# FFN steps: the next step's maxima and indices in the middle of a step, and the gathering of indices on GpSimd

## The reference

```python
sim = jnp.einsum('pbnhd,hkpd->pbnhk', q, keys)          # 2 halves x 8 heads x 32 keys
sx, ix = jax.lax.top_k(sim[0], TOPK)                    # TOPK = 8
sy, iy = jax.lax.top_k(sim[1], TOPK)
all_scores = (sx[..., :, None] + sy[..., None, :]).reshape(b, n, H, TOPK * TOPK)
all_indices = (ix[..., :, None] * NUM_KEYS + iy[..., None, :]).reshape(b, n, H, TOPK * TOPK)
scores, pk = jax.lax.top_k(all_scores, TOPK)
indices = jnp.take_along_axis(all_indices, pk, axis=-1)
wd = down_embed[indices]
wu = up_embed[indices]
h = gelu_new(jnp.einsum('bnd,bnhkd->bnhk', x, wd))
h = jax.nn.softmax(scores, axis=-1) * h
out = jnp.einsum('bnhk,bnhkd->bnd', h, wu)
```

## Time and profile before

| | kernel before |
|---|---|
| median of 3 executions | 1291.11 us |
| the profiled execution | 1291.46 us |
| its span, first to last instruction | 1289.7 us |
| PE busy | 1153.1 us (89%) |
| DVE busy | 1133.3 us (88%) |
| ACT busy | 876.8 us (68%) |
| POOL busy | 641.1 us (50%) |
| mean granted TensorE clock | 0.906 |

### The profile page before, as it was taken

How to read it: one execution, slowest core, us unless ns; L and a number is a source line. 1 busy time by engine, 2 the same in 40 slices (tenths; PEclk the granted TensorE clock), 3 DMA queues, 4 the chain that set the end, 5 groups by cost and what they waited for, 6 DMA issues and landing times. The chain is left out here.

```text
span 1289.7 us, 32620 instructions
## 1 busy us (share of the span) xinstructions
PE 1153.1 (89%) x12726; PEld 899.9 (70%) x12726; DVE 1133.3 (88%) x2851; ACT 876.8 (68%) x1227; POOL 641.1 (50%) x545
## 2 busy tenths in 40 slices
PE   6669899999999999999999999999997739888878
PEld 4537677777767777776777777677776628778778
DVE  7776799998999999899999989998986689999984
ACT  4858798888889888888988888898874332222211
POOL 5435667757576775757677575767241300000000
PEclk9789999999999999999999999999999676666666
DMA  4149799999999999999999999998996300000000
GB/s 161 25 103 200 165 197 191 194 186 201 199 199 200 197 193 195 195 198 205 194 195 194 194 195 199 175 201 169 196 189 133 86 0 2 5 6 6 5 5 6
DMA packets 665506, 185.73 MB, mean 144 GB/s; under 512 B 653923, under 2 KB 662279, under 8 KB 665223
## 3 DMA queue, kind: packets, MB, share of 16 engines
q1 hardware_dynamic: 665350, 183.64, 74.0%
HBM read 19.44 MB, written 0.82 MB: 16 GB/s over the span
## 5 line engine op out<-in xcount | busy, mean ns | idle before, releaser
L1021 ACT ACTIVATE e<-ps,bias 128x1444 f32<-128x1444 f32 (+1 forms) x208 | 305.7, 1470 | 136.0 <-DVE bias L1098 135.1
L1220 PE MATMUL ps<-pT,xa_hi 128*128 128x128 f16 x2288 | 382.0, 217 | 16.3 <-ACT uT L1044 16.2
L1224 PE MATMUL ps<-pT,xa_hi 128*128 128x128 f16 x2288 | 381.8, 217 | 3.4 <-DMA pT<-p 3.4
L1221 PE MATMUL ps<-pT,xa_lo 128*128 128x128 f16 x2288 | 382.1, 217 | 0.0
L1096 DVE TENSOR_REDUCE nmax<-ps 128x1 f32<-128x1444 f32 (+1 forms) x208 | 343.8, 1653 | 23.9 <-PE ps L1204 22.8
L1108 DVE TENSOR_TENSOR p<-e,p 128x1408 f16<-128x1408 f32 (+3 forms) x288 | 302.5, 1091 | 37.5 <-ACT p L1029 36.8
L1029 ACT ACTIVATE p<-e 128x1408 f16<-128x1408 f32 (+1 forms) x208 | 287.9, 1384 | 17.3 <-DMA pT<-p 3.7
L971 POOL TENSOR_TENSOR p<-e,p 128x1408 f16<-128x1408 f32 (+1 forms) x128 | 196.7, 1558 | 187.3 <-ACT p L1029 187.3
L1220 PEld LDWEIGHTS ps<-pT,xa_hi 128*128 128x128 f16 x2288 | 222.5, 98 | 43.4 <-issue 30.1
L1202 PE MATMUL ps<-xT_hi,q_hi 128*128 128x512 f16 (+1 forms) x624 | 230.8, 370 | 7.4 <-PEq L40 3.8
L1221 PEld LDWEIGHTS ps<-pT,xa_lo 128*128 128x128 f16 x2288 | 222.5, 98 | 13.1 <-issue 0.2
(11 more groups left out here) (248 smaller groups left out, 1920.1 us busy)
## 6 DMA issues: line engine op xcount, KB each, us to landing
raw<-in_ctx SPq DMA_DIRECT2D x16, 704.0 KB
pT<-p SPq DMA_TRANSPOSE x416, 3.7
f_wq<-in_L_ffn_w_q SPq DMA_DIRECT2D x1, 1024.0 KB, 5.3
f_wqt<-in_ffn_wq_t SPq DMA_DIRECT2D x2, 512.0 KB, 7.7
raw<-in_ctx SPq DMA_DIRECT2D x48, 18.0 KB
x_tok<-in_x SPq DMA_DIRECT2D x4, 200.0 KB
out_x<-ost SPq DMA_DIRECT2D x6, 128.0 KB, 1.8
wk_d<-in_wk_d SPq DMA_DIRECT2D x1, 512.0 KB, 5.8
```

The lines of the kernel that those rows point to most:

```text
L1021: act.activation(e32[t % E_BUF][rows, :], score_banks(t)[rows, 0:T], ACT.Exp, bias=bias[rows, t % N_BUF:t % N_BUF + 1]).then_inc(e_done, 1)
L1220: pe.matmul(out, hi, ph, start=n == 0, stop=False)
L1221: pe.matmul(out, lo, ph, start=False, stop=False)
L1224: pe.matmul(out, hi, pl, start=False, stop=False)
```

## The change

In `ffn`:

- The multiply of the mask by `idxw` and the three sums go from DVE to POOL (`gathered`), with the semaphore `gather` between them. POOL's order becomes `gathered(i)`, `norm_rstd(i-2)`, `combine(i+1)`; before it was `combine(i)`, `norm_rstd(i-2)`.
- All maxima, all indices and the cast to `idxf` of step i+1 now stand inside step i on DVE, between `weigh(i-1, 1)` and the wait for POOL's sums, and behind it: 32 maxima, 20 indices (`AHEAD`), and behind `sel` the other 12 and the cast. Those of step 0 stand ahead of the loop, in an order by halves of the tokens instead of halves of the scores.
- The four `weigh` and the parts of the last norm are spread anew over the step.
- ACT runs `picks(i)` first in a step, and `hidden(i, 1)` and `last_norm(i-2)` behind `esc`, ahead of `rT`.

In `front`, the load of `side` counts on `ld_k` with `wk_d` and `wq_t`, for which everything that waits for one of the three now waits, and `kb_done` is merged into `const_chain`.

The diff, cut to its core:

```diff
-        LD_W, LD_LATE, LD_K = 16 * 2, 16 * 2, 16 * 2
+        LD_W, LD_LATE, LD_K = 16 * 2, 16 * 2, 16 * 3
...
-            pool.wait_ge(ld_side, 16)
-            pool.tensor_scalar(sc1[:, :, :], side[:, :, :], 1.0, 1.0 / QA_SCALE, ALU.add, ALU.mult).then_inc(kb_done, 1)
+            pool.wait_ge(ld_k, LD_K)
+            pool.tensor_scalar(sc1[:, :, :], side[:, :, :], 1.0, 1.0 / QA_SCALE, ALU.add, ALU.mult).then_inc(const_chain, 1)
...
+            def gathered(i):
+                nh, w = step_shape(i)
+                na = nh * NB
+                pool.wait_ge(pick, 3 * i + 3)
+                pool.wait_ge(wide_idx, i + 1)
+                pool.tensor_tensor(out=eq[0:w, 0:na, :, :], in0=eq[0:w, 0:na, :, :], in1=idxw[0:w, 0:na, :, :], op=ALU.mult).then_inc(gather, 1)
+                pool.wait_ge(gather, 3 * i + 1)
+                pool.tensor_tensor(out=half4[0:w, 0:na, :, :], in0=eq[0:w, 0:na, 0:4, :], in1=eq[0:w, 0:na, 4:8, :], op=ALU.add).then_inc(gather, 1)
...
+            combine(0)
+            wide_rows(1)
             for i in range(NSTEP):
-                combine(i)
-                if i == 0:
-                    wide_rows(1)
+                gathered(i)
                 if i >= 2:
                     norm_rstd(i - 2)
+                if i + 1 < NSTEP:
+                    combine(i + 1)
...
             def picks(i):
-                act.wait_ge(pick, 7 * i + 1)
+                act.wait_ge(idxf_done, i + 1)
+                if i:
+                    act.wait_ge(gather, 3 * i - 2)
...
+                picks(i)
                 hidden(i, 0)
-                if i >= 2:
-                    last_norm(i - 2)
-                hidden(i, 1)
-                picks(i)
                 if i + 1 < NSTEP:
                     sims_out(i + 1)
                 act.wait_ge(dsc_done, i + 1)
                 act.activation(esc[0:w, 0:nh, :, :], dsc[0:w, 0:nh, :, :], ACT.Exp).then_inc(esc_done, 1)
+                hidden(i, 1)
+                if i >= 2:
+                    last_norm(i - 2)
                 act.wait_ge(selT_ps, i + 1)
...
-                dve.wait_ge(wide_idx, i + 1)
-                dve.wait_ge(pick, 7 * i + 4)
-                dve.tensor_tensor(out=eq[0:w, 0:na, :, :], in0=eq[0:w, 0:na, :, :], in1=idxw[0:w, 0:na, :, :], op=ALU.mult).then_inc(pick, 1)
                 dve.wait_ge(soft_done, 3 * i + 2)
...
+                if i:
+                    weigh(i - 1, 1)
+                if i >= 2:
+                    norm_stats(i - 2, 0)
+                if i + 1 < NSTEP:
+                    next_maxima(i + 1)
+                if i >= 2:
+                    norm_stats(i - 2, 1)
+                if i + 1 < NSTEP:
+                    next_indices(i + 1, 0)
+                if i >= 2:
+                    norm_stats(i - 2, 2)
+                if i:
+                    weigh(i - 1, 2)
                 dve.wait_ge(sel_done, 4 * i + 1)
...
                 dve.tensor_copy(sel[0:w, 0:2, 0:nh, :], erc[0:w, :, 0:nh, :]).then_inc(sel_done, 1)
+                if i + 1 < NSTEP:
+                    next_indices(i + 1, 1)
+                    next_cast(i + 1)
+                if i >= 2:
+                    norm_shift(i - 2)
                 if i:
                     weigh(i - 1, 3)
-
-                if i + 1 < NSTEP:
-                    dve.wait_ge(sim_done, i + 1)
-                    for n in range(EARLY):
-                        dve.max(top[0:step_shape(i + 1)[1], 0, n, :], simb[0:step_shape(i + 1)[1], 0, n, :])
-
                 dve.wait_ge(selT_done, 3 * i + 1)
...
+            next_maxima(0)
+            for part in range(2):
+                next_indices(0, part)
+            for k in range(1, NG):
+                centred(k)
+            dve.wait_ge(narrow_done, 1)
+            next_cast(0)
```

More of the change, by code:

```diff
@@ L82, in front @@
         ld_x = [sem(f"ld_x{c}") for c in range(NG)]
-        ld_w, ld_late, ld_k, ld_side = (sem(n) for n in ("ld_w", "ld_late", "ld_k", "ld_side"))
+        ld_w, ld_late, ld_k = (sem(n) for n in ("ld_w", "ld_late", "ld_k"))
         const_chain = sem("const_chain")
@@ L94, in front @@
         kf_ps, kf_done, qa_ps, qa_hi_done, qa_lo_done = (sem(n) for n in ("kf_ps", "kf_done", "qa_ps", "qa_hi_done", "qa_lo_done"))
[L95 removed]
+        kb_ps, kbar_done = sem("kb_ps"), sem("kbar_done")
         q0_ps, q0_taken, q0_hi = sem("q0_ps"), sem("q0_taken"), sem("q0_hi")
@@ L278, in q0_out @@
                 if g == 0:
-                    act.wait_ge(kb_done, 2)
+                    act.wait_ge(const_chain, 13)
                 for j in range(4):
@@ L1256 @@
 NSTEP = -(-NT // STEP_TOK)
-EARLY = 6
+AHEAD = 20
 PAD = P + 4
@@ L1340, in ffn @@
         sim_ps, sim_done, top_done, comb_done, best_done = (sem(n) for n in ("sim_ps", "sim_done", "top_done", "comb_done", "best_done"))
+        idxf_done, gather = sem("idxf_done"), sem("gather")
         dsc_done, esc_done, pick, sel_done, selT_ps, selT_done = (sem(n) for n in ("dsc_done", "esc_done", "pick", "sel_done", "selT_ps", "selT_done"))
@@ L1430, in norm_rstd @@
                 pool.tensor_tensor(out=frs[0:w, 0:nh], in0=fve[0:w, 0:nh], in1=nhalf[0:w, 0:nh], op=ALU.pow).then_inc(z_rstd, 1)
+            def gathered(i):
[6 more added lines that the diff above has]
+                pool.tensor_tensor(out=half4[0:w, 0:na, :, :], in0=eq[0:w, 0:na, 0:4, :], in1=eq[0:w, 0:na, 4:8, :], op=ALU.add).then_inc(gather, 1)
+                pool.wait_ge(gather, 3 * i + 2)
+                pool.tensor_tensor(out=half2[0:w, 0:na, :, :], in0=half4[0:w, 0:na, 0:2, :], in1=half4[0:w, 0:na, 2:4, :], op=ALU.add).then_inc(gather, 1)
+                pool.wait_ge(gather, 3 * i + 3)
+                pool.tensor_tensor(out=ij[0:w, 0:nh, :, :].rearrange("s a n k -> s (a n) k"), in0=half2[0:w, 0:na, 0, :], in1=half2[0:w, 0:na, 1, :],
+                                   op=ALU.add).then_inc(sel_done, 1)
+            combine(0)
+            wide_rows(1)
             for i in range(NSTEP):
-                combine(i)
-                if i == 0:
-                    wide_rows(1)
+                gathered(i)
                 if i >= 2:
                     norm_rstd(i - 2)
+                if i + 1 < NSTEP:
+                    combine(i + 1)
             norm_rstd(NSTEP - 2)
@@ L1631, in norm_shift, with next_maxima, next_indices, next_cast @@
                                          op0=ALU.mult, op1=ALU.mult).then_inc(fnm_done, 1)
+            def next_maxima(i):
+                nh, w = step_shape(i)
+                if i:
+                    dve.wait_ge(sim_done, i)
+                    dve.wait_ge(comb_done, i)
+                    dve.wait_ge(top_done, 2 * i)
+                    dve.sem_inc(f_waited, 1)
+                for hf in range(nh):
+                    for n in range(NB):
+                        if not i and n % FH == 0 and hf == 0:
+                            dve.wait_ge(first_done, n // FH + 1)
+                            dve.sem_inc(f_waited, 1)
+                        ins = dve.max(top[0:w, hf, n, :], simb[0:w, hf, n, :])
+                ins.then_inc(top_done, 1)
+            def next_indices(i, part):
+                nh, w = step_shape(i)
+                if part == 0:
+                    dve.wait_ge(top_done, 2 * i + 1)
+                    dve.wait_ge(idxf_done, i)
+                    dve.sem_inc(f_waited, 1)
+                for k in range(*((0, min(AHEAD, nh * NB)), (min(AHEAD, nh * NB), nh * NB))[part]):
+                    hf, n = divmod(k, NB)
+                    ins = dve.max_index(idx[0:w, hf, n, :], top[0:w, hf, n, :], simb[0:w, hf, n, :])
+                    if k == nh * NB - 1:
+                        ins.then_inc(top_done, 1)
+            def next_cast(i):
+                nh, w = step_shape(i)
+                dve.wait_ge(top_done, 2 * i + 2)
+                dve.wait_ge(wide_idx, i)
+                dve.tensor_copy(idxf[0:w, 0:nh, :, :], idx[0:w, 0:nh, :, :]).then_inc(idxf_done, 1)
             def step(i):
@@ L1635, in step @@
                 j, na, nb = nh * HK, nh * NB, nh * NC
[L1636 to L1677, removed]
                 dve.wait_ge(comb_done, i + 1)
@@ L1694, in step @@
                 if i:
-                    weigh(i - 1, 2)
+                    weigh(i - 1, 0)
                 dve.wait_ge(best_done, 2 * i + 2)
@@ L1699, in step @@
                 dve.tensor_scalar(pij[0:w, 0:nh, 1, :], flat, K8 - 1, None, ALU.bitwise_and).then_inc(pick, 1)
-                dve.wait_ge(pick, 7 * i + 2)
+                dve.wait_ge(pick, 3 * i + 1)
                 dve.tensor_copy(pijf[0:w, 0:nh, :, :], pij[0:w, 0:nh, :, :]).then_inc(pick, 1)
@@ L1704, in step @@
                 dve.tensor_reduce(ssum[0:w, 0:nh, :], esc[0:w, 0:nh, :, :], AX_X, ALU.add).then_inc(soft_done, 1)
-                dve.wait_ge(pick, 7 * i + 3)
+                dve.wait_ge(pick, 3 * i + 2)
                 dve.tensor_tensor(out=eq[0:w, 0:na, :, :],
```

4 lines of the change are left out of this document (2 added, 2 removed).

## The result

The changed kernel takes 1298.96 us (median of four executions, 1297.85 to 1302.47) against 1290.86 us of the kernel before beside it: a ratio of 1.0068, 95% interval 1.005 to 1.0087. Run once more, beside the experiments, it gave 1.0074 (1.0049 to 1.0099). It is slower, by about twice what was forecast: 8.1 us in place of 4.0. The profiled execution took 1302.47 us with a span of 1300.7.

What follows compares the result with a forecast made beforehand. VectorE was taken to bound the kernel, by little over TensorE. Steps 0 to 6 summed 5.1 + 0.1 + 0.67 + 0.73 + 0.77 - 2.76 - 0.6 = +4.0 us, from 1291.1 to 1295.1 us; range 1284 to 1300.

Steps and rivals of the forecast that it cites:

- third rival: Steps 2 to 4: GpSimd's `comb` gets ahead of VectorE's `eu`, which loses 2.1 us a step; 1301.4 us, chance 11%.
- The stall of `sel`: VectorE's `sel`, behind the mask, stands while GpSimd's two-input multiply holds the shared read path: 3.9 us.
- M: Time of GpSimd's multiply of 2048 elements with two inputs, taken at 2.03 ns an element: 4.16 us.
- first rival: `sel` doesn't stand behind GpSimd's multiply; steps 1 to 5 fall to TensorE's floor; 1279.2 us, chance 12%.
- second rival: GpSimd reads f16 fast: multiply of 1.90 us, `sel` stall of 1.65 us; 1283.8 us, chance 7%.
- Steps 2 to 4: Stretch from first expert matmul to `oneh` becomes 24.95 us: +0.67, +0.73 and +0.77 us.
- one-input instructions go on: VectorE instructions with one input aren't held by GpSimd's two-input work, as indices kept pace under `comb`; no cost.
- Step 1: Stretch to `oneh` in the step without norms: +3.9 - 2.65 - 1.15 = +0.1 us.
- step 5: Only 16 maxima and 16 indices follow, so the stretch falls to TensorE's floor of 21.36 us: -2.76 us.
- step 6: TensorE's 0.54 us idle ahead of `turned` goes: -0.6 us.
- Step 0: `esc` comes 3.44 us earlier, but step 1's maxima, indices and cast stand ahead of the first `oneh`: +5.1 us.
- The last norm: `last_norm` stands ahead of `rT` in ScalarE's queue and waits for `fnm`: 0.43 us more from step 2 on.

Runs made afterwards that it cites:

- the version with `comb` late: Against the changed kernel, GpSimd's `comb` of the next step also waits until VectorE has written `sel`; 1295.03 us, 1.0037 to the kernel before.
- the version with `sel` first: Against the changed kernel, `srec` and `sel` move ahead of the mask `eq`, nothing else; 1283.7 us, 0.9934 to the kernel before.

## Why the prediction was right, and where it was short

- *The whole.* The direction and the larger of the two stalls were forecast. The 1298.96 us lie in the range of 1284 to 1300, but near its end, and the same kernel took 1300.58 when run again, past it. The upper part of the range was there for the third rival, and what came was a collision with `comb`, if not the one it named. That part of the outcome is luck.
- *The stall of `sel`.* Right in cause, place and size: GpSimd first by 0.12 us as worked out, `sel` 4.09 us long against 4.2, M = 4.06 against 4.16. Taking it away turned the loss into a gain, as the first rival said; that rival's 1279.2 was 4.5 us too good, since the second stall stays (22.3 us a step, not 21.36). The second rival, f16 read fast, fell with M.
- *Steps 2 to 4.* This is the step that failed. They rose by 2.59, 2.32 and 2.35 us, not by 0.67, 0.73 and 0.77: 5.1 of the 5.5 us by which the stage missed the forecast (9.5 against 4.0, below). (The terms as written add up to 24.98, not 24.95; that changes nothing here.) The sentence that failed is "one-input instructions go on". It rested on indices under `comb`, and was taken to hold for every instruction with one input. `erc` has one input too and stands: 1.7 us a step, which the version with `comb` late gives back (1.6 of it). The sum had this term at nothing. The rest in step 2, 0.35 us, is the wait ahead of `dsc`, and its cause is open. The page named there, the Trainium skill's SBUF — State Buffer, "Who interferes with whom", lists copy, cast and `tensor_scalar` beside the two-input operations; the forecast used only the half of the rule that it had a row for.
- *The third rival* saw the collision: `comb` goes behind `fve` and `eu` is beside it. It asked about `eu` alone, and `eu` was first, by 0.25 us (1127.99 against 1128.24). The two instructions behind it were not asked about. Its size was near, 2.1 us for what became 1.7, and its 1301.4 is nearer to the measured 1298.96 than the forecast's 1295.1.
- *Step 1* (-0.05 against +0.1), *step 5* (21.50 against 21.36) and *step 6* (-0.36 against -0.6): right. Step 5 goes to TensorE's floor, and so does every full step once both stalls are gone.
- *Step 0.* +5.1 forecast. The second half of the first scores and what VectorE does with it, before and after:

```profile
1025.86 1.59 DVE L1647 MAX8 top<-simb 128x8 f32<-128x32 f32 x16 [4.46 <-ACT simb L1461]
...
1027.38 2.33 DVE L1664 MAX8 top<-simb 128x8 f32<-128x32 f32 x24 [5.20 <-ACT simb L1478]
```

  The first expert matmul went from 1064.40 to 1071.15, 6.75 us; 1.52 of them were there already at these maxima, so the step itself cost 5.23. The terms of ScalarE came out as forecast: `esc` reaches VectorE at 1043.54, less 1.52 is 1042.02, against 1041.85. But that the total is within 0.13 us is in part luck. The forecast took step 0 of the kernel before from one execution, and that depends on TensorE's clock: against the 24.49 us of the run with the edit of `front` alone, the 31.43 of the changed kernel would be a cost of 6.9.
- *The sum.* In the stage 5.23 - 0.05 + 2.59 + 2.32 + 2.35 - 2.62 - 0.36 = 9.5 us in the profiled execution, against a difference of the medians of 8.1. The 1.52 us ahead of the stage come on top in this one execution; the front edit alone has a ratio of 0.9996, and the changed kernel itself, run again, had these maxima 2.18 us earlier.
- *The last norm.* The 0.43 us show as the wait of `oneh` for `rT` (0.44 in the row at 1134.12). `ost`, ahead of `rT` in the queue, is what it waits for:

```profile
1133.11 0.81 ACT L1526 ACTIVATE ost<-ps,fnm,frs 128x128 f32<-128x128 f32 x2 [12.74 <-DVE fnm L1649]
1133.81 0.28 ACT L1545 ACTIVATE rT<-ps 128x128 f16<-128x128 f32 x1
```

The idea of the change, then, was sound. The kernel with the same work on GpSimd and an order that keeps the two engines off one path is 0.9% faster than the one before, and by the two ratios about 1.6% faster than the changed one. The order alone, with nothing more on GpSimd, gives 0.3% of it.

## What to carry to other kernels

When work goes to GpSimd, list every VectorE instruction that will start under it, and ask of each not how many inputs it has but whether it reads SBUF over both paths: two inputs there, or one input at two elements a cycle. Put the short ones ahead of the instruction that releases GpSimd; let those run beside it that were seen to be free (maxima, indices, and the instructions listed below that read PSUM). A row for one kind of instruction doesn't speak for another of the same count of inputs: the pace of the instruction (here 0.14 us for 128 elements from SBUF, 0.21 from PSUM) hints at which kind it is.

## What the runs showed of the hardware

- One-input `tensor_scalar` and casts from SBUF to SBUF stand behind a running two-input instruction of GpSimd, until it ends (1.08 and 1.10 us for 0.23; a cast 1.08 us for 0.29). GpSimd was first by only 0.06 us there (1128.24 against 1128.30). With the input in PSUM the same `tensor_scalar` is not held: 0.29 us.
- A waiting VectorE instruction gets its turn between the two halves of `comb`: each `erc` lost one half, not both.
- Not held under GpSimd's two-input work: MAX8 and FIND_INDEX8, as before, the norm's statistics, which read PSUM (0.28 to 0.29 us under the multiply in the version with `sel` first), and `wgt`, which has one input in PSUM and one in SBUF: in step 6 of that version it started 1.73 us into the 2.13 us of the multiply and took 0.69. `eu`, with two inputs in SBUF, took its usual 0.28 us beside the root, which works 0.71 us on two elements: the length of that GpSimd instruction was not the length for which it held the path, if it held it at all.
- f16 is no faster than f32 on GpSimd with two inputs: 4.06 us for 2048 elements, 2.17 for 1024, 1.98 to 2.12 ns an element, as 2.03 in the earlier trace rows.
- The granted clock of TensorE differed between executions in the same instructions (0.57 and 1.00 over the scores' matmuls of step 0), and moved a path that no change had touched by 1.7 us.
